# Pass 0 of a macaron block: sum over tokens on TensorE, rounding straight from PSUM, and new places for the work of all engines

## The chip, the cores and the metric

The kernel runs on one core of one Trainium2 chip. The metric is the device time of one execution in microseconds, as the median over runs. Lower is better.

## What is computed

The reference is one macaron block on x of 4 sequences with 1024 tokens and 128 features: half a feed-forward step, a mixer, and half a feed-forward step.

```python
x = x + 0.5 * ffn(layernorm(x))
x = x + attn(layernorm(x))
x = x + 0.5 * ffn(layernorm(x))
```

The feed-forward step has 8 experts of width 512. It is routed by sequence, not by token:

```python
seq_rep = hidden_states.mean(axis=1)
probs = softmax(seq_rep @ gate_w)
top_w, top_i = top_k(probs, 2)            # normalised to sum 1
hmid = gelu(hidden_states @ w1[e] + b1[e])  # for the two chosen e
out += combine[:, e] * (hmid @ w2[e] + b2[e])
```

The mixer (`attn`) is an RMS norm, a causal convolution of 4 taps, SiLU, one projection into dt, v and gate, softplus and clips of dt, a rotary turn of v, a decayed cumulative sum in chunks of 32 tokens with carries between the chunks, a mix over heads, the gate and an output projection. Everything is float32.

## The kernel before

**Passes and slots.** The two feed-forward steps of 4 sequences are 8 passes (pass q works on sequence q % 4). A pass has 8 slots: two chosen experts with four blocks of 128 hidden features each. A slot has an up product (`up`, L830: weights 128x128, z of 1024 columns) into one of two buffers `hid_ps`, a gelu on ScalarE (`gelu`, L628), and a down product into `y_ps` (`down`). The up product is made of three terms, since both factors are split into a rounded high part and the rest (`z_hi`, `z_lo`, `w1_hi`, `w1_lo`, all of the faster type float32r): 3 terms in 2 halves are 6 matmuls. The down product has three forms: by parts, with the gelu's output split too (ScalarE rounds it at L635, VectorE subtracts at L1194; 6 matmuls, L881), whole in float32 (4 matmuls, L881), and, in passes 1 to 4, with tokens as rows (L856, 16 matmuls).

**Before a pass.** VectorE takes statistics of each of the 8 tiles of 128 tokens (L1064, L1067), GpSimd adds epsilon and takes the power -0.5 (`rstd_of`, L454, L456), VectorE normalises into `f_tok` (L1079), TensorE transposes tile by tile into `aux_ps` (`turn`, L923), ScalarE copies from there to `f_tok`, whose accumulator gives the sum over tokens `zsum` (`turn_z`, L553 to L560), and rounds the copy into `z_hi` (L564); VectorE makes `z_lo` (`split_z`, L1087). VectorE widens the sum to 128 columns (`widen_sum`, L1133, L1136) so that TensorE can multiply it with the router's weights (`pre_route`, L939; L1014 in pass 0), and picks the two experts (`route`, L1143 to L1153). ScalarE, VectorE and SyncE load the two indices into registers (`value_load`); SyncE then fetches the experts' weights (`load_experts`).

In pass 0 all this stands on an idle chip. The first 256 columns of w1 of all experts are loaded ahead (`w1_all`), and ScalarE and VectorE split the first expert's from there after the register loads (`split_first`, L582, L1100); the other half comes by DMA after the index (`w1_first`, split at L598 and L1111). TensorE multiplies constants (`WARM_EARLY` = 13 products at L1009 before the first transpose, `WARM` = 5 at L1018 behind the router product), whose results nobody reads. Every float32 product with 128 weights shows as two instructions in the trace.

**The mixer** of a sequence lies between the token passes. Its names: `mixer_rms` (GpSimd's additions and the power for both norms in one operation of 16 columns, L500), `mixer_affine`, `mixer_normalise` (L1255), `mixer_residual` (eight operations on ScalarE, L673), `mixer_cos` (L1335, two halves), `mixer_decay`, `mixer_scan` and others.

**The order of work** on each engine is written out by hand or by a planner in the table `AT`: for each engine and kind of work a tick for each pass, sequence or slot. A slot has 40 ticks: `up(s)` and `gelu(s)` stand at tick 40 (s + 1), `down(s)` at 40 s + 98 or, by parts, 40 s + 132. Each engine goes through the ticks in order, and its queue is strictly in that order; the semaphores only make it wait. Before the table's first tick stand pass 0's preparation and routing. `aux_ps` is one buffer, shared by transposes, router and the mixer's products; `take_aux` makes each user wait for the last reader of the one before.

## Time and profile before

| | us |
|---|---|
| median of 3 runs | 264.93 |
| lowest and highest run | 263.94, 265.67 |
| the profiled execution, its own time | 265.42 |
| its span from the first to the last instruction | 263.6 |

Busy in the span: TensorE 96%, VectorE 84%, ScalarE 78%, GpSimd 29%. The mean granted clock of TensorE is 0.987 of full speed.

How to read it: the busy share of TensorE is that of an engine whose matmuls are pipelined, so 96% says that it seldom waited, not that it ran at its peak. The chain of waits is followed back from the last instruction to what released each step; an engine's share of it says more than its busy time. The granted clock is 1.00 at 2.4 GHz and 0.50 at 1.2 GHz. Times in the rows are counted from the start of the span.

### The profile page before, as it was taken

The numbers are of one execution on the slowest core, as the hardware profiler recorded it, in microseconds if no ns is written. First come the engines' busy times: TensorE is split into PE (matmuls) and PEld (weight loads), VectorE is DVE, ScalarE is ACT, GpSimd is POOL, SyncE is SP. The second block draws the span as 40 slices with busy tenths as digits, with TensorE's granted clock in tenths as the row PEclk, the third lists the DMA queues.
The fourth block names the chain that finished last, engine by engine and source line by source line (L and its number), as shares of the span: only waits on it lengthen the run. The fifth ranks groups of instructions, "written<-read, shape, count | busy, mean of one in ns | idle before, by whom it ended". The sixth has DMA issues, their size and how long they took to land.

```text
span 263.6 us, 4451 instructions
## 1 busy us (share of the span) xinstructions
PE 252.1 (96%) x1442; PEld 211.9 (80%) x1442; DVE 221.6 (84%) x555; ACT 204.6 (78%) x247; POOL 75.9 (29%) x84
## 2 busy tenths in 40 slices
PE   7699997999999999999999999999999999999995
PEld 6477785999979988989978999778866678887885
DVE  3668986979899998999899999899999998666632
ACT  1349899569797977877977968999989877879750
POOL 6130215550295506562015617200314004000000
PEclk9859999999999999999999999999999999999999
DMA  6589237056000061000600000600006000372022
GB/s 192 171 263 332 86 101 298 24 239 261 2 0 0 2 216 46 4 0 0 240 22 1 2 0 0 232 10 2 2 0 216 23 2 0 115 207 80 0 80 80
DMA packets 16630, 23.42 MB, mean 89 GB/s; under 512 B 1184, under 2 KB 11680, under 8 KB 16608
## 3 DMA queue, kind: packets, MB, share of 16 engines
q1 hardware_dynamic: 15296, 22.33, 25.4%
q10 hardware_dynamic: 1232, 0.55, 0.7%
q8 instruction: 11, 0.18, 0.3%
q0 software_dynamic: 80, 0.26, 0.3%
q14 instruction: 11, 0.09, 0.1%
...
## 4 chain that ended last, share of the span: by engine, by line
PE 70%; DVE 10%; issue 7%; ACT 6%; POOL 3%; DMA 1%; ACTq 1%; SPq 0%; DVEq 0%; POOLq 0%
PE hid_ps L830 27%; PE y_ps L856 18%; PE y_ps L881 12%; PE aux_ps L923 3%; PE aux_ps L970 3%; PE aux_ps L1002 2%; PE aux_ps L991 2%; POOL f_rstd L456 1%; PE aux_ps L951 1%; ACT hid L628 1%; ACT late L718 1%; DMA xt<-x_dram 1%; PE hid_ps L900 1%; DVE hid_lo L1194 1%; PE y_ps L900 1%
## 5 line engine op out<-in xcount | busy, mean ns | idle before, releaser
L830 PE MATMUL hid_ps<-z_hi,w_parts 128*128 128x512 f32 x256 | 85.4, 418 | 0.7 <-ACT w_parts L582 0.7
L628 ACT ACTIVATE hid<-hid_ps,w_sb 128x1024 f32<-128x1024 f32 x56 | 61.7, 1111 | 19.1 <-PE hid_ps L830 18.6
L856 PEld LDWEIGHTS y_ps<-w_sb,hid 128*128 128x128 f32 x512 | 61.4, 192 | 4.0 <-issue 1.2
L856 PE MATMUL y_ps<-w_sb,hid 128*128 128x128 f32 x512 | 62.6, 275 | 0.6 <-ACT hid L628 0.6
L830 PEld LDWEIGHTS hid_ps<-z_hi,w_parts 128*128 128x128 f32 x256 | 46.8, 193 | 11.6 <-issue 2.4
L830 PE MATMUL hid_ps<-z_lo,w_parts 128*128 128x512 f32 x128 | 40.9, 402 | 0.0
L1194 DVE TENSOR_TENSOR hid_lo<-hid,hid_hi 128x1024 fp32r<-128x1024 f32 x25 | 30.2, 1220 | 8.2 <-ACT hid_hi L635 8.0
L830 PEld LDWEIGHTS hid_ps<-z_lo,w_parts 128*128 128x128 f32 x128 | 24.6, 192 | 5.8
L635 ACT ACTIVATE hid_hi<-hid 128x1024 fp32r<-128x1024 f32 x25 | 26.1, 1056 | 1.5 <-PE y_ps L881 1.2
L454 POOL TENSOR_SCALAR f_ve<-f_mv 128x8 f32<-128x8 f32 (+1 forms) x9 | 4.5, 495 | 66.0 <-DVE f_mv L1067 66.0
L479 POOL TENSOR_SCALAR bias_tok<-w_sb,coef 128x128 f32<-128x128 f32 x8 | 6.2, 786 | 44.4 <-DVE coef L1163 34.1
L1079 DVE TENSOR_SCALAR f_tok<-xt,f_mv,f_rstd 128x128 f32<-128x128 f32 x64 | 17.2, 341 | 1.2 <-POOL f_rstd L456 1.2
L1064 DVE BATCH_NORM_STATS2 f_stat<-xt 128x6 f32<-128x128 f32 x64 | 13.3, 277 | 3.8 <-DMA xt<-x_dram 3.7
L1265 DVE SCALAR_TENSOR_TENSOR xc<-xs,vec_sb,xc 128x1024 f32<-128x1024 f32 x12 | 15.4, 1279 | 1.2 <-ACT xc L681 1.1
L881 PE MATMUL y_ps<-hid_hi,w_hi 128*128 128x512 f32 x50 | 16.3, 407 | 0.0
L881 PE MATMUL y_ps<-hid_lo,w_hi 128*128 128x512 f32 x50 | 15.6, 394 | 0.5 <-DVE hid_lo L1194 0.5
L881 PE MATMUL y_ps<-hid_hi,w_lo 128*128 128x512 f32 x50 | 15.6, 394 | 0.0
L456 POOL TENSOR_TENSOR f_rstd<-f_ve,neg_half 128x8 f32<-128x8 f32 (+1 forms) x9 | 14.2, 1578 | 0.8
L500 POOL TENSOR_TENSOR m_inv<-m_var,neg_half 128x16 f32<-128x16 f32 x4 | 13.8, 3446 | 0.3
L520 POOL TENSOR_SCALAR small<-mix_tmp 128x32 f32<-128x32 f32 x4 | 5.8, 1456 | 25.5 <-DVE cumd L1308 25.5
L673 ACT ACTIVATE xt<-xt,m_shift,m_gain 128x128 f32<-128x128 f32 x32 | 12.7, 482 | 0.0
L881 PEld LDWEIGHTS y_ps<-hid_lo,w_hi 128*128 128x128 f32 x50 | 9.3, 188 | 3.1 <-DVE hid_lo L1194 1.0
(143 smaller groups left out, 463.3 us busy)
## 6 DMA issues: line engine op xcount, KB each, us to landing
...
```

What stands on the lines that cost most here:

```text
L456: nc.gpsimd.tensor_tensor(f_rstd[:, tiles], f_ve[:, tiles], neg_half[:, 0, tiles], ALU.pow).then_inc(done, 1)
L500: nc.gpsimd.tensor_tensor(m_inv[:, :, :], m_var[:, :, :], neg_half[:, :, :], ALU.pow).then_inc(m_pool_step, 1)
L628: nc.scalar.activation(hid[:, slot % HBUF, :], hid_ps[:, slot % 2, :], ACT.Gelu, bias=bias).then_inc(hid_ready, 1)
L635: nc.scalar.activation(hid_hi[:, slot % 2, :], hid[:, slot % HBUF, :], ACT.Copy).then_inc(hid_hi_ready, 1)
L673: nc.scalar.activation(xt[:, b, t, :], xt[:, b, t, :], ACT.Identity, bias=m_shift[:, t:t + 1], scale=m_gain[:, t:t + 1]).then_inc(x_plus_h, 1)
L830: last = nc.tensor.matmul(hid_ps[:, slot % 2, cols], w, z[:, q % 2, cols], start=first, stop=end)
L856: last = nc.tensor.matmul(y_ps[:, cols], hid[:, slot % HBUF, cols], w_sb[:, q % 2, k, W2_AT + f * P:W2_AT + (f + 1) * P], start=t == 0 and ...
L881: last = nc.tensor.matmul(y_ps[:, cols], wt, src[:, cols], start=t == 0 and i == 0, stop=slot + 1 in (SLOTS * (q + 1), TAIL[0]) and end)
L1064: V.bn_stats(f_stat[:, t, :], xt[:, b, t, :]).then_inc(f_stats_step, 1)
L1079: V.tensor_scalar(f_tok[:, t, :], xt[:, q % B, t, :], f_mv[:, t, 0:1], f_rstd[:, t:t + 1], ALU.subtract, ALU.mult).then_inc(f_norm_done, 1)
L1194: V.tensor_tensor(hid_lo[:, slot % 2, :], hid[:, slot % HBUF, :], hid_hi[:, slot % 2, :].bitcast(F32), ALU.subtract).then_inc(hid_lo_ready, 1)
L1265: V.scalar_tensor_tensor(xc[:, :], xs[:, k:k + N], conv_w[:, k:k + 1], xc[:, :], ALU.mult, ALU.add).then_inc(conv_step, 1)
```

## The change

- **Pass 0, variance.** VectorE adds epsilon behind the statistics of each half; GpSimd only takes the two powers.
- **Pass 0, sum and transposes.** TensorE computes the sum over tokens itself: for each tile a product with the tile as weights and one column of ones, summed over the eight tiles in `y_ps`, ahead of the tile's transpose. Behind each transpose but the last stands a product of constants with 64 columns. VectorE copies the one-column sum (`keep_sum`).
- **Pass 0, z.** ScalarE rounds from PSUM into `z_hi` by halves (`turn_first`), VectorE subtracts from PSUM by halves (`split_z_first`): the first half ahead of `keep_sum`, the second behind the routing. The first up product waits for the halves one by one.
- **Register loads.** In `split_first`, ScalarE and VectorE load the second index behind the first expert's splits.
- **Passes 1 to 7.** `widen_sum` is gone: TensorE reads the sum as a broadcast. ScalarE's next turn waits for the router product instead, and VectorE's normalisation for the transposes.
- **Mixer.** GpSimd takes the power that `mixer_normalise` needs first, alone, and then the other one (5 steps in place of 4). `mixer_cos` is one operation of 1024 columns.
- **WARM** is 9 in place of 5.
- **Places.** The table `AT` is rewritten for all engines. Examples: pass 2's transposes move from 366 to 415, right behind the last down product of pass 0 (tick 412), with VectorE's normalisation from 351 to 410; the transposes of pass 0's output from 415 to 429, behind the first slot of pass 1; the splits of all experts' w1 on ScalarE from 184 and later to 290 and later; `mixer_residual` from 580, 980, 1340, 1616 to 896, 1248, 1420, 1984; `mixer_affine` of sequence 3 from 1548 to 1892; the transposes of pass 5's output from 2206 to 2326.

```diff
-        "f_norm": {1: 206, 2: 366, 3: 769, 4: 1129, 5: 1489, 6: 1860, 7: 2146},
+        "f_norm": {1: 206, 2: 415, 3: 809, 4: 1169, 5: 1469, 6: 1815, 7: 2126},
-        "y_turn_y": {0: 415, 5: 2206, 6: 2446, 7: 2600},
+        "y_turn_y": {0: 429, 5: 2326, 6: 2466, 7: 2600},
...
-        "m_residual": {0: 580, 1: 980, 2: 1340, 3: 1616},
+        "m_residual": {0: 896, 1: 1248, 2: 1420, 3: 1984},
...
-    WARM_EARLY, WARM = 13, 5
+    WARM_EARLY, WARM = 13, 9
...
-                nc.gpsimd.tensor_tensor(m_inv[:, :, :], m_var[:, :, :], neg_half[:, :, :],
+                nc.gpsimd.tensor_tensor(m_inv[:, 1, :], m_var[:, 1, :], neg_half[:, 1, :],
                                         ALU.pow).then_inc(m_pool_step, 1)
+                nc.gpsimd.tensor_scalar(m_var[:, 0, :], m_mv[:, :, 1], LN_EPS, None, ALU.add).then_inc(m_pool_step, 1)
+                pool.wait_ge(m_pool_step, POOL_STEPS * b + 3)
+                nc.gpsimd.tensor_tensor(m_inv[:, 0, :], m_var[:, 0, :], neg_half[:, 0, :],
+                                        ALU.pow).then_inc(m_pool_step, 1)
...
+            def turn_first():
+
+                act.wait_ge(f_turned_head, 1)
+                nc.scalar.activation(z_hi[:, 0, 0:HALF], aux_ps[:, 0:HALF], ACT.Copy).then_inc(zhi_head, 1)
+                act.wait_ge(f_turned, 1)
+                nc.scalar.activation(z_hi[:, 0, HALF:], aux_ps[:, HALF:], ACT.Copy).then_inc(zhi_ready, 1)
...
-                chosen.extend(act.value_load(top_i[0:1, k:k + 1], min_val=0, max_val=E - 1) for k in range(TOP))
+                chosen.append(act.value_load(top_i[0:1, 0:1], min_val=0, max_val=E - 1))
                 for f in range(HEADS):
...
+                chosen.append(act.value_load(top_i[0:1, 1:2], min_val=0, max_val=E - 1))
...
-            pre_norm(0)
+            take_aux(zlo_ready, 1, 2)
+            for t in range(NT):
+                pe.wait_ge(f_norm_done, t + 1)
+                last = nc.tensor.matmul(y_ps[:, 0:1], f_tok[:, t, :], ones[:, 0:1], start=t == 0, stop=t == NT - 1)
+                if t == NT - 1:
+                    last.then_inc(zsum_up, 1)
+                last = nc.tensor.transpose(aux_ps[:, t * P:(t + 1) * P], f_tok[:, t, :], ident[:, :])
+                if t % (NT // 2) == NT // 2 - 1:
+                    last.then_inc(f_turned_head if t < NT // 2 else f_turned, 1)
+                if t < NT - 1:
+                    nc.tensor.matmul(hid_ps[:, 0, 0:P // 2], ones[:, :], ones[:, 0:P // 2], start=True, stop=True)
             pe.wait_ge(small_in, 16)
-            pe.wait_ge(zwide_ready, 1)
-            nc.tensor.matmul(y_ps[:, HALF:HALF + E], zsum_wide[:, :], gate_sb[:, :],
+            pe.wait_ge(zsum_ready, 1)
+            nc.tensor.matmul(y_ps[:, HALF:HALF + E], zsum[:, 0:1].broadcast_to([P, P]), gate_sb[:, :],
                              start=True, stop=True).then_inc(logits_up, 1)
...
             pass_stats(0)
             pass_normalise(0)
-            widen_sum(0)
+            split_z_first(0)
+            keep_sum()
             route(0)
-            split_z(0)
+            split_z_first(1)
             split_first()
             coefficients(0)
```

## Rows read from the trace of the kernel before

**Rows 1.** The page: TensorE's granted clock in 40 equal slices, in tenths.
```profile
PEclk9859999999999999999999999999999999999999
```

**Rows 2.** Busy time by stage: stretch, length, then busy us (instructions) by engine, clock, DMA.
```profile
core 0: us, PE busy (x) PEld busy (x) DVE busy (x) ACT busy (x) POOL busy (x), PEclk, DMA share, GB/s
...
40.00:143.00 103.00, 101.24 (x672) 89.50 (x671) 93.63 (x230) 82.53 (x102) 45.05 (x44) 1.00 0.23 87
...
143.00:212.00 69.00, 66.77 (x361) 53.57 (x360) 67.02 (x149) 61.03 (x69) 17.98 (x16) 1.00 0.14 47
...
213.90:255.40 41.50, 41.46 (x199) 33.90 (x198) 27.08 (x61) 33.86 (x37) 2.80 (x2) 1.00 0.26 77
```

**Rows 3.** Chain that ended last, its start: start us, us, engine and line.
```profile
8.35 1.11 PE aux_ps L923 x4
9.49 0.70 ACT f_tok L556 x2
10.21 0.36 DVE zsum_wide L1136
10.70 0.37 PE y_ps L1014 x2
...
11.64 0.48 ACTq L579
12.40 0.28 ACTq L579
13.05 0.32 ACT w_parts L582
13.41 5.35 PE hid_ps L830 x12
...
20.48 2.75 PE hid_ps L830 x12
```

**Rows 4.** Busy time by stretch at the start, columns as in rows 2.
```profile
6.36:10.70 4.34, 2.10 (x8) 1.13 (x9) 2.58 (x9) 1.80 (x5) 1.47 (x3) 1.00 0.86 278
10.70:13.41 2.71, 2.04 (x12) 1.75 (x13) 1.61 (x5) 0.99 (x3) 0.00 (x0) 0.67 0.01 2
13.41:18.48 5.07, 5.07 (x12) 4.02 (x13) 3.96 (x26) 1.96 (x6) 1.65 (x2) 0.50 0.87 248
```

**Rows 5.** Timeline from 6 to 15 us: start us, us, engine, line, operation [idle before].
```profile
6.85 1.07 POOL L456 TENSOR_TENSOR f_rstd<-f_ve,neg_half 128x4 f32<-128x4 f32 x1
...
7.95 1.12 DVE L1079 TENSOR_SCALAR f_tok<-xt,f_mv,f_rstd 128x128 f32<-128x128 f32 x4 [0.17 <-POOL f_rstd L456]
...
11.53 1.22 DVE L1087 TENSOR_TENSOR z_lo<-f_tok,z_hi 128x1024 fp32r<-128x1024 f32 x1
...
14.70 0.42 ACT L598 ACTIVATE w_parts<-m_tok 128x256 fp32r<-128x256 f32 x1 [0.86 <-DMA m_tok<-wpack_dram]
```

**Rows 6.** Chain that ended last, near its end, where TensorE's queue is full.
```profile
222.28 0.87 PE aux_ps L923 x8
...
225.94 0.12 PE aux_ps L939 x2
```

**Rows 7.** Two lines of the kernel: duration in ns, least, median and most.
```profile
L1133 DVE TENSOR_SCALAR zsum_wide<-ones,zsum x7: 264/281/286, 28.5 to 225.0; 128x128 f32<-128x128 f32 x7
...
L1335 DVE TENSOR_TENSOR late<-aux_ps,rope_sb x8: 666/684/691, 78.5 to 193.4; 128x512 f32<-128x512 f32 x8
```

**Rows 8.** Timeline at the end of pass 0, TensorE.
```profile
44.91 1.09 PE L951 MATMUL aux_ps<-ident,yt 128*128 128x128 f32 x8 [1.36 <-ACT yt L659]
```

**Rows 9.** Around the last residual block: busy time, and ScalarE's timeline there and later.
```profile
171.00:175.00 4.00, 4.00 (x21) 2.78 (x20) 3.38 (x7) 3.89 (x11) 0.00 (x0) 1.00 0.08 30
...
171.38 3.18 ACT L673 ACTIVATE xt<-xt,m_shift,m_gain 128x128 f32<-128x128 f32 x8
...
212.79 1.21 ACT L659 ACTIVATE yt<-y_ps,bias,coef 128x1024 f32<-128x1024 f32 x1 [1.34 <-DVE bias L1206]
```

**Rows 10.** The page's groups: gelu and rounding of its output; busy us, mean ns.
```profile
L628 ACT ACTIVATE hid<-hid_ps,w_sb 128x1024 f32<-128x1024 f32 x56 | 61.7, 1111 | 19.1 <-PE hid_ps L830 18.6
...
L635 ACT ACTIVATE hid_hi<-hid 128x1024 fp32r<-128x1024 f32 x25 | 26.1, 1056 | 1.5 <-PE y_ps L881 1.2
```

250 lines of the change are left out of this document (118 added, 132 removed), and 6 rows, old and new, of the table AT.

## The prediction

> **What bounds the kernel now.** I read the page's busy shares first: TensorE is busy for nearly the whole span, and its granted clock is full except in the third and fourth of forty slices [rows 1]. Then I cut the span into stages. From 40 to 143 us TensorE works 101.2 of 103 us, from 213.9 to 255.4 us all of the time; between them, from 143 to 212 us, VectorE works 67.0 of 69 us and TensorE 66.8, so both are nearly full there, and TensorE's idle time in all three stages is only 4.0 us [rows 2]. What happens in those stages is therefore mostly a queue that is worked off: a matmul that starts earlier at the front lets the end come earlier by the same amount, unless VectorE or ScalarE stops it on the way.
>
> The front is different. In the chain of waits the first expert matmul starts at 13.41 us, behind a serial relay: transpose, ScalarE's copy with its sum, VectorE's widening, the router product, the index, two register loads, ScalarE's rounding of the first weights [rows 3]. And the clock is at its lower level, 1.2 GHz, for all of the first twelve expert matmuls: 0.67 on average from 10.70 to 13.41 us, 0.50 until 18.48 us, and 1.00 before and after [rows 4]. These twelve take 5.35 us; twelve of the same kind take 2.75 us from 20.48 us on, at 2.4 GHz [rows 3]. Before the fall TensorE had been busy 2.10 of 4.34 us, with eight transposes and nothing else [rows 4]. So the start holds two things that a change could win: the relay, and 2.6 us of low clock. The low digits of the clock stand in the trace of this one execution; in others the fall may stand elsewhere.
>
> **The change, part by part.**
>
> *Variance plus epsilon on VectorE in pass 0.* GpSimd's own addition and its two hand-overs go; its two powers then stand nearly back to back. The second power starts at 6.85 us today [rows 5] and ends 1.07 us later; the first ends about 6.55 us. With one more small operation on VectorE ahead of each power I expect the last normalised tile 0.2 us earlier, at 8.85 us in place of 9.07 us (7.95 + 1.12) [rows 5]. The bounds are 0 and 0.3 us.
>
> *The sum over tokens on TensorE, products as fill.* Each of eight tiles now costs TensorE a one-column product with the tile as weights (two instructions, as every f32 product here), the transpose, and a 64-column product (two instructions). Eight transposes take 0.87 us in a full queue, so 0.11 us each; a two-instruction product of 8 columns adds 0.12 us [rows 6]. A product with 1 column I take at 0.12 us, one of 64 columns at 0.12 us as well (bounds 0.12 and 0.22 us, from the 8-column row and from two instructions of 128 columns at the transposes' pitch). That makes 0.35 us a tile, where VectorE delivers one each 0.28 us (1.12 / 4) [rows 5]. TensorE becomes the slower of the two: from about 6.95 us, 8 x 0.35 - 0.12 = 2.7 us later, the last tile's sum and transpose have been issued (9.65 us), and they are out at about 9.8 to 9.9 us. Today the last transpose is out at 9.46 us (8.35 + 1.11) [rows 3]. So this part by itself makes the transposes 0.4 us later (0 to 1.0 us later with the bounds), and pays it back in the relay: ScalarE's 0.70 us and the 128-wide widening of 0.36 us [rows 3] leave the path, and a copy of one column (about 0.2 us with its hand-over, as the small chain steps) takes their place. The router product then starts at 9.8 + 0.2 + 0.14 = 10.1 us in place of 10.70 us. VectorE's first half of the low part, about 0.68 us like the other 128x512 reads of PSUM [rows 7], stands ahead of that copy in its queue; it needs ScalarE's rounding of the first half, and ends at about 9.8 us, just as the sum does. That is the closest race of this step: if it is late, the router is late by as much. The second half, after the routing operations, ends by about 11.7 us, before the matmuls want it.
>
> *Rounding straight from PSUM.* ScalarE no longer copies z and then rounds it, and no longer reads an accumulator. This is hidden: two activations of 512 columns, about 0.60 us each without the accumulator's read, end at about 10.5 us, and the matmuls start later than that.
>
> *The second register load moved behind the first weights.* From 11.64 us to 12.40 us ScalarE's queue has one register load, from 12.40 us to 13.05 us the other, and then the rounding starts [rows 3]. The later one leaves the path: 0.65 us. From the router product on, the relay is 0.94 us to the load (11.64 - 10.70), 0.76 us for it, 0.36 us to the matmul (13.41 - 13.05), so the first expert matmul starts at 10.1 + 0.94 + 0.76 + 0.36 = 12.2 us: 1.2 us earlier. The load itself then stands before the first bias copies, which only the first gelu needs.
>
> *Four more constant products behind the router.* Eighteen instructions at 0.11 us are 2.0 us, so from 10.3 to 12.3 us at full clock: they just fill the gap and may cost 0.1 us. At half clock they would take twice that (see the rivals).
>
> *The clock.* After the change TensorE has a gap of about 0.6 us around 6.4 to 7.0 us, another short one at 9.9 us, and work at all other times from 1.7 us on. Today its longest thin stretch is the one before the fall: 2.10 of 4.34 us from 6.36 us, then nothing of length until 10.9 us [rows 4]. I take it that the clock now stays at 2.4 GHz. Then the twelve matmuls run from 12.2 to 14.95 us. What is late next is ScalarE: it waits for the rest of the first expert's weights until 14.70 us today [rows 5], and that transfer follows the index, so 14.1 us; 0.42 us for the rounding [rows 5] and 1.11 us for the first gelu [rows 10] make 15.65 us; the first down product takes 1.72 us (20.48 - 18.76, where 18.76 is the end of the twelve) and ends at 17.4 us. Today it ends at 20.48 us [rows 3]. **Gain at the start: 3.0 us**; without the clock 1.2 us. The later weights, which VectorE waited for today ahead of its other splits, are waited for after them in the new order, so I see no stall of the size of the gain behind this.
>
> The Trainium skill ("TensorE: Matmul & The Clock Gate", Part 4: PE-mode transpose) says that a transpose doesn't count as busy for the clock. The trace agrees as far as it goes: the fall came after a stretch that held transposes only. By that rule the sum would get less help from the new mix, where transposes are a third of the time; that is the second case below.
>
> *The end of pass 0.* TensorE idles 1.36 us for the scaled output, which ScalarE makes in 1.21 us [rows 8, 9]. The transposes of pass 2 (0.87 us) now stand right there, and those of the output go behind the first token slot. The transposes are gated by VectorE's normalisation, which is placed there too (twice 1.12 us for eight tiles [rows 5]), so they will not fit wholly into the hole: 0.4 us, bounds 0 and 0.87 us.
>
> *Widening gone in passes 1 to 7, cosine in one piece.* Seven operations of 281 ns are 2.0 us of VectorE, and per batch two of 684 ns become one of about 1.22 us, 0.15 us less [rows 5, 7]. The broadcast read of the sum costs TensorE nothing new. Only where VectorE is full does this count: two widenings and one or two cosines lie between 143 and 212 us. 0.6 us, bounds 0 and 1.2 us.
>
> *The mixer's power in two.* VectorE's normalisation then waits for a power of 8 columns in place of one of 16, and two steps sooner. In the two stages where the mixer runs VectorE idles 11.4 us in all [rows 2], and the waits list none of it for this power, so by itself it gives nothing (lower bound); GpSimd, busy 29% of the span, hides what it costs. Its worth is the freer placement.
>
> *The rewritten places.* Nearly every tick moves. Most move by a slot or less, with their consumers. Of size: the residual blocks, eight operations, 3.18 us of ScalarE in one piece [rows 9], go later by 316, 268, 80 and 368 ticks (a slot has 40). I count the rest at nothing, between 1.5 us better and 1.5 us worse.
>
> The sum: 3.0 + 0.4 + 0.6 = 4.0 us. The profiled execution took 265.42 us, so 261.4 us. It lies 0.5 us above the median of the runs (264.93 us), whose own start I can't see; I predict **261.2 us**. About 1%, or 2.65 us, is what a measurement of this kernel can tell from no change.
>
> **The rivals.**
>
> *A. The forecast*, 261.2 us, 50%, with 259.3 to 262.8 us around it from the bounds of the terms.
>
> *B. The clock falls anyway near the first expert matmuls.* Only the 1.2 us of the relay remain: 264.9 - 1.2 - 1.0 = 262.7 us. For it: the one-column products and the short fill stream few columns, and the mean of 0.67 puts today's fall near 11.6 us, while the five products ran [rows 4]. Against it: TensorE has hardly a gap left. 20%.
>
> *C. The clock falls before the nine products.* Then the fill itself is in the way: 18 x 0.21 = 3.8 us from 10.3 to 14.1 us, the twelve end at 14.1 + 5.35 = 19.45 us, 0.7 us later than the 18.76 us of today. With the 1.0 us from elsewhere: 264.6 us. The full clock in the thin stretch of today's run speaks against it. 10%.
>
> *D. The gain is swallowed between 143 and 212 us.* VectorE idles 2.0 us in 69 there [rows 2]; if its order, not TensorE's, sets the path, only what VectorE itself starts earlier is kept. Against it: it idles 9.4 us in the 103 us before, so it can come forward with TensorE. Half of the start lost: 262.8 us. 12%.
>
> *E. Slower: the residual blocks stall TensorE.* ScalarE needs 1.1 us for the gelu and 1.1 us for the split [rows 10] against TensorE's 2.8 us a slot (twice the 1.37 us of six matmuls), so a block of 3.18 us in one slot can leave TensorE waiting up to 3.18 - 0.6 = 2.6 us, and there are four. It decides from 1.0 us each on (that eats the 4.0 us). Full price 264.9 - 4.0 + 4 x 1.8 = 268.1 us, with 1.8 us for a slot whose gelu is a little ahead. Against it: around today's last block TensorE is busy 4.00 of 4.00 us [rows 9], and the last one now goes near 212 us, where ScalarE idles 1.34 us by itself [rows 9]; it also leaves ScalarE's full stretch. 8%.
>
> **How the numbers follow.** A has 50%, B 20%, D 12%, C 10%, E 8%. The range 259.2 to 265.2 us holds A, B, D, C, without E and the tails. Faster by over 1% means below 262.3 us: most of A and a third of B and D, 0.6. Within 1%: 0.32. Slower by over 1% (267.6 us): 0.08.
>
> **What the profile would show.** Right: first expert matmul at 12.2 us; granted clock 1.00 from 5 to 20 us and the first twelve in 2.8 us; first down product finished near 17.4 us; TensorE idle less than 1.0 us around the end of pass 0; the end of the matmuls of pass 7 some 4 us earlier. Wrong: clock below 1.00 between 9 and 18 us (B, C); TensorE idle over 6 us from 40 to 255 us (D, E); ScalarE as the releaser of long waits beside the residual blocks (E); the router product later than 10.4 us, if the PSUM halves or the one-column products cost more than taken.

## The result and the profile after

| | us |
|---|---|
| before, median of 10 runs beside the change | 264.68 |
| after, median of 10 runs | 267.39 |
| after, lowest and highest run | 264.88, 268.00 |
| after, the profiled execution, its own time | 265.35 |
| its span | 263.6 |

The ratio of after to before is 1.0091, with a 95% interval from 1.0062 to 1.0120. The change makes the kernel slower by 0.9%, where 1.4% faster was forecast.

One property of the runs is needed for every number below. Executions of one kernel differ in their mean granted clock: 1.000, 0.993 or 0.987 of full speed, because a fall of the clock happens in some executions and not in others. I call them "at full clock", "at 0.993" and "at 0.987". Medians of all executions, us (number of executions):

| | full clock | 0.993 | 0.987 |
|---|---|---|---|
| before (118 executions, run beside the experiments) | 263.43 (15) | 264.38 (39) | 265.12 (64) |
| after | 265.12 (2) | 266.49 (3) | 267.80 (5) |

So the change loses 1.7 us at equal full clock (by only two executions of after), and 2.7 us where both have the lowest mean. The profiled execution of after is one of the two at full clock, and the profiled one of before has 0.987. Two traces with nearly the same own time (265.35 and 265.42 us) therefore hide a difference of 1.7 us.

The page of after: span, busy time by engine, and the clock in 40 slices.

```profile
span 263.6 us, 4512 instructions
...
PE 254.0 (96%) x1480; PEld 214.1 (81%) x1480; DVE 221.3 (84%) x547; ACT 203.6 (77%) x244; POOL 78.9 (30%) x86
...
PEclk9999999999999999999999999999999999999999
```

The clock stays full at the start, where it fell before [rows 1]. The front in stretches: busy us (instructions) by engine, then the granted clock.

```profile
core 0: us, PE busy (x) PEld busy (x) DVE busy (x) ACT busy (x) POOL busy (x), PEclk, DMA share, GB/s
6.36:10.70 4.34, 4.04 (x41) 3.88 (x40) 3.04 (x10) 0.60 (x1) 1.19 (x2) 1.00 0.92 300
10.70:13.51 2.81, 2.63 (x25) 2.47 (x24) 1.24 (x6) 1.03 (x3) 0.00 (x0) 1.00 0.04 13
13.51:18.20 4.69, 4.39 (x19) 2.84 (x18) 3.55 (x24) 3.39 (x9) 0.88 (x2) 1.00 0.74 195
```

Against [rows 4] the clock is 1.00 in all three. The first twelve expert matmuls run from 13.51 to 16.52 us, so 3.0 us in place of 5.35 us [rows 3]. The first down product has its last matmul out at 18.78 us in place of 20.48 us:

```profile
15.91 0.61 PE L831 MATMUL hid_ps<-z_hi,w_parts 128*128 128x512 f32 x2
16.82 1.96 PE L882 MATMUL y_ps<-hid,w_sb 128*128 128x512 f32 x4 [0.30 <-ACT hid L625]
```

But the first of them starts at 13.51 us, not 1.2 us earlier than the 13.41 us of before. The relay up to it, from the timeline (start us, us, engine, line, operation, and in brackets the idle time before and its releaser):

```profile
10.98 0.16 DVE L1154 COPY zsum<-y_ps 128x1 f32<-128x1 f32 x1 [0.55 <-PE y_ps L1012]
...
11.28 0.36 PE L1022 MATMUL y_ps<-gate_sb,zsum 128*128 128x8 f32 x2 [0.18 <-DVE zsum L1154]
...
11.96 0.17 DVE L1167 FIND_INDEX8 top_i<-top_v,y_ps 128x8 uint32<-128x8 f32 x1
...
13.08 0.51 ACT L578 ACTIVATE w_parts<-late 128x128 fp32r x2 [1.34 <-DVE top_i L1167]
...
13.51 0.71 PE L831 MATMUL hid_ps<-z_hi,w_parts 128*128 128x512 f32 x2
```

The router product starts at 11.28 us; before it started at 10.70 us [rows 3], and 10.1 us was forecast. The second register load is gone from the way as expected: from the index (12.13 us) to the rounding are 0.95 us. From the router product to the first expert matmul it is 2.23 us; before it was 2.71 us (10.70 to 13.41), and 2.06 us was forecast. What ate the gain lies ahead of the router: the eight tiles. TensorE's groups there, one row for each line of code (busy us, mean ns of one, idle before):

```profile
L1012 PE MATMUL y_ps<-ones,f_tok 128*128 128x1 f32 x16 | 2.7, 238 | 0.3 <-DVE f_tok L1093 0.3
L1015 PE MATMUL aux_ps<-ident,f_tok 128*128 128x128 f32 x8 | 2.5, 306 | 0.0
L1019 PE MATMUL hid_ps<-ones 128*128 128x64 f32 x14 | 2.3, 248 | 0.0
```

These are 2.7 + 2.5 + 2.3 = 7.5 us of overlapping busy time in 4.1 us. The timeline shows the pitch: the transposes start at 7.24, 7.75, 8.25, 8.76 us and so on, 0.51 us apart, where I had 0.35 us. Within a tile the one-column product takes 0.20 us of it (7.55 to 7.75), the transpose 0.14 us (to 7.89) and the 64-column product 0.17 us (to 8.06).

Then the middle. The longest single piece of TensorE's idle time and what leads to it:

```profile
82.49 4.34 POOL L519 TENSOR_SCALAR small<-mix_tmp 128x32 f32<-128x32 f32 x1 [2.73 <-DVE cumd L1325]
...
86.93 0.41 POOL L520 TENSOR_SCALAR ncd<-cumd 128x32 f32<-128x32 f32 x1
...
87.42 2.04 POOL L523 TENSOR_TENSOR small<-ncd 128x31 f32<-128x31 f32 x1
...
89.55 0.26 ACT L728 ACTIVATE small_e<-small 128x64 f32<-128x64 f32 x1 [2.93 <-POOL small L523]
...
91.12 1.11 ACT L625 ACTIVATE hid<-hid_ps,w_sb 128x1024 f32<-128x1024 f32 x1
...
92.38 2.02 PE L857 MATMUL y_ps<-w_sb,hid 128*128 128x128 f32 x16 [2.98 <-ACT hid L625]
```

TensorE waits 2.98 us for a gelu. The gelu waits in ScalarE's queue behind a small operation of the mixer's decay (L728), which waits 2.93 us for GpSimd, whose first operation here took 4.34 us.

### The profile page after: what moved, and what is told of

It is laid out like the page before. It is cut to its first block, busy times and chain, and to the rows that moved or that the text cites. A ratio compares the mean times of both kernels' runs of the same rounds, so it can differ in the third digit from the quotient of the medians.

```text
span 263.6 us, 4512 instructions
## 1 busy us (share of the span) xinstructions
PE 254.0 (96%) x1480; PEld 214.1 (81%) x1480; DVE 221.3 (84%) x547; ACT 203.6 (77%) x244; POOL 78.9 (30%) x86
## 4 chain that ended last, share of the span: by engine, by line
PE 43%; DVE 8%; issue 3%; DVEq 0%
PE hid_ps L831 16%; PE y_ps L882 12%; PE y_ps L857 6%; PE aux_ps L968 3%; PE aux_ps L924 2%; PE aux_ps L989 1%; PE hid_ps L901 1%; PE y_ps L901 1%; PE aux_ps L949 1%; DVE xc L1282 1%; DVE late L1383 1%; DVE m_tok L1272 1%; PE aux_ps L1000 1%; DVE xt L1400 1%; DVE f_stat L1072 1%
## 5 line engine op out<-in xcount | busy, mean ns | idle before, releaser
L831 PE MATMUL hid_ps<-z_hi,w_parts 128*128 128x512 f32 x256 | 83.8, 411 | 0.0
L831 PEld LDWEIGHTS hid_ps<-z_hi,w_parts 128*128 128x128 f32 x256 | 46.1, 189 | 11.0 <-issue 2.4
L831 PE MATMUL hid_ps<-z_lo,w_parts 128*128 128x512 f32 x128 | 40.0, 394 | 0.0
L1211 DVE TENSOR_TENSOR hid_lo<-hid,hid_hi 128x1024 fp32r<-128x1024 f32 x25 | 30.3, 1220 | 10.2 <-ACT hid_hi L632 10.1
L831 PEld LDWEIGHTS hid_ps<-z_lo,w_parts 128*128 128x128 f32 x128 | 24.0, 188 | 5.6
L463 POOL TENSOR_SCALAR f_ve<-f_mv 128x8 f32<-128x8 f32 x7 | 1.7, 249 | 64.8 <-DVE f_mv L1075 64.6
L453 POOL TENSOR_TENSOR f_rstd<-f_ve,neg_half 128x8 f32<-128x8 f32 (+1 forms) x9 | 15.0, 1663 | 2.6 <-DVE f_ve L1079 1.9
L519 POOL TENSOR_SCALAR small<-mix_tmp 128x32 f32<-128x32 f32 x4 | 7.7, 1920 | 26.2 <-DVE cumd L1325 26.2
L475 POOL TENSOR_SCALAR bias_tok<-w_sb,coef 128x128 f32<-128x128 f32 x8 | 7.6, 958 | 17.7 <-DVE coef L1180 17.5
L882 PEld LDWEIGHTS y_ps<-hid_hi,w_lo 128*128 128x128 f32 x50 | 9.4, 188 | 2.3
```

The costliest lines, as they stand in the source:

```text
L453: nc.gpsimd.tensor_tensor(f_rstd[:, tiles], f_ve[:, tiles], neg_half[:, 0, tiles], ALU.pow).then_inc(done, 1)
L831: last = nc.tensor.matmul(hid_ps[:, slot % 2, cols], w, z[:, q % 2, cols], start=first, stop=end)
L882: last = nc.tensor.matmul(y_ps[:, cols], wt, src[:, cols], start=t == 0 and i == 0, stop=slot + 1 in (SLOTS * (q + 1), TAIL[0]) and end)
L1211: V.tensor_tensor(hid_lo[:, slot % 2, :], hid[:, slot % HBUF, :], hid_hi[:, slot % 2, :].bitcast(F32), ALU.subtract).then_inc(hid_lo_ready, 1)
```

## Experiments

The runs ask four things: what the clock at the start is worth, what the new relay costs and gives, which of the new places lose the rest, and how. "New table" is the `AT` of after, "old table" that of before. For every kernel I give the ratio to before with its interval, and medians at equal clock where that decides.

**1. The table against the code.** `old_table` is the changed code with the old table. `new_table` is the code of before with the new table (and the widening placed just ahead of each routing).

```diff
-AT = {...of after...}
+AT = {...of before...}        # old_table
```


> All code of the changed kernel, but the table of places is that of the kernel before. Theory P (the places lose it: ScalarE's decay step of sequence 0, placed ahead of a gelu, waits 2.9 us for GpSimd, and TensorE then idles 3.0 us at 89 us, in every execution): the stall is gone; TensorE idles under 1 us from 80 to 100 us, and the kernel is 2 to 3 us faster than the changed one, ratio to before 0.995 to 1.000. Theory F (the front loses it: five weight loads a tile, and a low clock after it): nothing of the 2.7 us against before comes back; ratio to before 1.005 to 1.015, as with the new places.

> All code of the kernel before, but the table of places is the changed one (the widening, which that table lacks, is placed a few ticks ahead of each router product). Theory P: slower than before by about the stall less the 0.9 us that the end of pass 0 gives, ratio 1.005 to 1.012, and TensorE idles 2.5 to 3.5 us near 90 us. Theory F: within 0.3% of before.

`old_table`: 264.79 us (264.03 to 265.54, 12 runs), ratio 1.0009 [0.9984, 1.0034], 11 of 12 at full clock. `new_table`: 267.78 us (266.29 to 268.76, 6 runs), ratio 1.0121 [1.0080, 1.0162]. In the medians the new places alone, on unchanged code, make the whole loss. The changed code with old places loses nothing and wins nothing, although its clock is held, which alone is worth more than a microsecond (experiment 4). At equal clock it has a loss of its own: 264.76 us at full clock against 263.43 us of before, and after is only 0.4 us above that. So at full clock the new places cost the changed code little on balance (experiment 6 shows good and bad blocks in them); what they add is mostly that 8 of 10 executions fall below full clock, against 1 of 12 with the old places. On the code of before the new places cost more: 266.73 us (two executions) against 264.38 us at 0.993.

The stall of 2.98 us isn't needed for this loss. In `new_table` the same decay operation stands ahead of the same gelu, but GpSimd's first operation takes 2.40 us and TensorE waits 0.34 us for the gelu; that expectation failed. Its longest waits behind the first expert matmuls are for the widened sum (waits of TensorE, us in total, times, longest):

```profile
PE aux_ps L939 <- DVE zsum_wide L1133: 1.2, 2, 0.8
PE y_ps L856 <- ACT hid L628: 0.3, 1, 0.3
```

In the trace of `old_table` TensorE waits in pass 0 for a split on VectorE that in the old table stands behind the bias of the down product (tick 107 ahead of 112). The bias reads the down product's weights, which are fetched at that time; the row of the bias itself names no releaser, so that it waits for this transfer is argued, not shown:

```profile
19.28 0.21 DVE L1222 TENSOR_SCALAR bias2a<-w_sb,coef 128x1 f32<-128x1 f32 x1 [1.79 <-issue]
...
20.14 1.20 PE L832 MATMUL hid_ps<-z_hi,w_parts 128*128 128x512 f32 x4 [0.38 <-DVE w_parts L1134]
```

**2. The decay of sequence 0 behind the gelu.** One number: ScalarE's decay from tick 830 to 860, with gelu(20) at 840.

```diff
-        "m_decay": {0: 830, 1: 1100, 2: 1533, 3: 1906},
+        "m_decay": {0: 860, 1: 1100, 2: 1533, 3: 1906},
```


> The changed kernel with one number changed: ScalarE's decay step of sequence 0 at tick 860 in place of 830, so behind the next slot's gelu. Theory P: the wait for GpSimd remains, but no gelu stands behind it; TensorE idles under 1 us near 90 us; 2 to 3 us faster than the changed kernel, ratio to before 0.997 to 1.002. Rival R (the path then runs on through the same late decay step to the scans, and VectorE, not TensorE, sets the end): less than 1 us comes back. Theory F: nothing comes back.

265.52 us (264.69 to 266.24, 12 runs), ratio 1.0038 [1.0014, 1.0061]. The wait of 2.98 us is gone. The clock is full in 9 of 12 executions (2 of 10 in after) and never at 0.987. But at full clock the median is 265.43 us, not below after's 265.12 us. The gelu no longer waits; instead the mixer's own scan is late and TensorE waits for that (waits of TensorE, us in total, times, longest):

```profile
PE aux_ps L1000 <- DVE late L1391: 1.2, 1, 1.2
PE aux_ps L989 <- DVE late L1383: 0.8, 1, 0.8
```

So the stall costs nothing that its cure gives back at equal clock: the two traces end the last matmul at the same 260.71 us. Its price is the clock: after with the stall falls to 0.993 or 0.987 in 8 of 10 executions, without it 3 of 12 fall, to 0.993.

**3. Without the seven products behind the tiles** (`no_fill`), to test the 0.51 us a tile and the clock.

```diff
-                if t < NT - 1:
-                    nc.tensor.matmul(hid_ps[:, 0, 0:P // 2], ones[:, :], ones[:, 0:P // 2], start=True, stop=True)
```


> The changed kernel without the seven constant products between the transposes. Theory F1 (weight loads set the pitch: 0.51 us a tile for five): 0.34 us a tile for three, so the last sum is ready 1.1 us earlier and the first expert matmul starts at 12.4 us in place of 13.5 us; 1 us faster at the same clock. Theory F2 (the fill holds the clock up): the clock falls in all executions, for longer than now, mean granted clock 0.986 or less, and the median is not better than that of the changed kernel.

265.58 us (265.12 to 267.01, 12 runs), ratio 1.0053 [1.0027, 1.0080]. A tile now takes 0.29 us, which is VectorE's pace (0.28 us), and the first expert matmul starts at 12.28 us, 1.23 us earlier than in after: two weight loads less for each of seven tiles. At a mean of 0.993 it is 1.2 us faster than after (265.30 against 266.49 us). But no execution has a full mean. In the profiled one the clock holds at the start and falls right behind the stall:

```profile
86.00:91.13 5.13, 2.14 (x10) 1.50 (x9) 4.54 (x5) 3.01 (x4) 1.99 (x1) 0.99 0.63 195
91.13:94.54 3.41, 3.41 (x17) 3.41 (x17) 2.90 (x3) 3.41 (x6) 0.00 (x0) 0.52 0.53 212
94.54:98.00 3.46, 3.46 (x25) 2.97 (x23) 1.28 (x1) 3.46 (x10) 0.65 (x3) 1.00 0.00 0
```

TensorE was busy 2.14 of 5.13 us, then ran 3.41 us at about the lower level while it was full of work, and rose again. Each such fall costs about 1.4 us here (after: 265.12, 266.49 and 267.80 us for none, one and two steps of mean clock). Where the eight lower executions of after fall isn't shown, since its profiled one has the full clock. And the start isn't safe without the seven products: in the profiled executions of `early` and `mixed_no_fill` (experiments 5 and 6), which leave them out too, the granted clock is 0.50 from 10.8 to 14.2 us.

**4. Only constant products added to before** (`before_filled`): seven of 64 columns between pass 0's transposes, three of 128 columns behind them, nine behind the router in place of five.

```diff
+                    if head_done is not None and t < NT - 1:
+                        nc.tensor.matmul(hid_ps[:, 0, 0:P // 2], ones[:, :], ones[:, 0:P // 2], start=True, stop=True)
...
+            for _ in range(3):
+                nc.tensor.matmul(hid_ps[:, 0, 0:P], ones[:, :], ones[:, :], start=True, stop=True)
             pe.wait_ge(small_in, 16)
             pe.wait_ge(zwide_ready, 1)
```


> The kernel before, all places and the relay as they were, with constant products alone added: seven of 64 columns between pass 0's transposes, three of 128 behind them, and nine in place of five behind the router product. Theory C (the clock is worth what the executions of before say: 263.5 us at a mean clock of 0.999 or 1.000, 265.2 us at 0.987): the clock is full in most executions and the median is 263.4 to 264.0 us, ratio to before 0.995 to 0.998, better than all the changed code with the old table. Theory N (the full clock is worth no more than the 0.6 us seen with the changed code): 264.5 to 265 us.

263.70 us (263.34 to 264.03, 10 runs), ratio 0.9957 [0.9936, 0.9977], all ten at full clock. This is the cleanest price of the clock at the start. Before's own executions at full clock and at 0.987 differ by 265.12 - 263.43 = 1.7 us; `before_filled` is 1.4 us under before at 0.987. The twelve matmuls are stretched by more, 2.3 us (5.35 less 3.0). Both traces start the first expert matmul at 13.41 us, and from slot 4 on `before_filled` stands 1.8 to 1.9 us ahead of before's trace, to the end. I use it as the reference at full clock from here on.

**5. New places in front, old ones behind.** `mixed` takes a place from the new table only where both tables have it at tick 600 or earlier; `mixed_no_fill` leaves out the seven products too, and `old_no_fill` is the old table without them.

> The changed kernel, with its new places only where the old and the new tick are both at or below 600 (pass 0 and 1), and the old places behind. Theory S (the new places of pass 0 win, the ones behind put VectorE's scan of sequence 0 ahead of the convolution of sequence 1 and lose it again): the first 20 slots are 2 to 2.5 us earlier than before, as in the changed kernel, and at least 1 us of it is kept to the end; ratio to before 0.990 to 0.997. Theory M (the mixer's chain sets the end in any order, and the front can't move it): no more than 0.3 us at slot 24 and at the end; ratio 0.998 to 1.003.

> As before this, and without the seven constant products between the transposes. Both theories: the first expert matmul 1.1 us earlier. Theory S: 0.5 to 1.1 us faster than with them, ratio to before 0.986 to 0.994. Theory M: the same end as with them.

> The changed code with the old table of places and without the seven products between the transposes. Theory G (weight loads on TensorE's path are what the front paid): 1.0 us earlier from slot 0 on, the clock still at its full level in most executions since the stall at 89 us isn't there, and 0.5 to 1.0 us faster than with the products; ratio to before 0.996 to 0.999. Theory K (without the products the clock falls at the start in most executions, as before the change): mean clock 0.987 to 0.993 in most, no faster than before.

| | median, us (range, runs) | ratio to before | at full clock |
|---|---|---|---|
| `mixed` | 265.95 (265.19 to 266.49, 12) | 1.0052 [1.0030, 1.0074] | 265.81 |
| `mixed_no_fill` | 264.17 (263.81 to 265.59, 12) | 0.9978 [0.9958, 0.9998] | 263.99 |
| `old_no_fill` | 263.71 (263.25 to 264.27, 11) | 0.9963 [0.9943, 0.9983] | 263.61 |

The seven products cost 1.2 us with the old table (264.76 less 263.61) and 1.8 us with the mixed one: what they delay at the start stays to the end. `mixed` was a miss: I expected it to keep the start's gain, and it waits for VectorE in the slots 16 to 19, where new and old places meet. A table of places can't be halved at a tick without new waits at the seam; `mixed` measures its seam too.

**6. One block of places at a time.** All without the seven products. `order_back`: the new table with the old order of sequence 0's scan and sequence 1's convolution. `early`: the old table, with new places only up to tick 250. `early_end`: `early` and in addition the new places at the end of pass 0. `early_two`: `early` with products behind tiles 4 and 6, 14 in place of 13 products ahead of the tiles and 7 in place of 9 behind the router. `new_behind`: `early` in front, old places up to 600, new places behind. `output_first`: the new table, but pass 0's output transposes ahead of the first slot of pass 1 as before.

```diff
# early_end against early
-        "f_norm": {1: 206, 2: 366, ...
+        "f_norm": {1: 206, 2: 415, ...
-        "y_turn_y": {0: 415, ...
+        "y_turn_y": {0: 429, ...
...
# output_first against no_fill
-        "y_turn_y": {0: 429, ...
+        "y_turn_y": {0: 415, ...
```


> The changed kernel without the seven products between the transposes and with all its new places, but for sequence 0's decay exponential, scans, gate, heads, output and sequence 1's clip, first tap and convolution, which have the old ticks: so the convolution of sequence 1 stands ahead of the scan of sequence 0 again, and the decay step behind the gelu. Theory O (that order lost the 3 us between slots 20 and 24): no stall of 3 us, and slot 24 starts at least 2 us earlier than in the same kernel with the new order at its full clock; 1.0 to 2.5 us faster than it (265.3 us at 0.993, 266.9 us at 0.987), ratio to before 0.990 to 0.998. Theory M (the mixer's chain as a whole): slot 24 within 0.5 us of where it is now; then only the lower clock behind the stall comes back, 264.0 to 264.5 us.

> The changed code without the seven products, the old places, but the new ones where both ticks are at or below 250: VectorE's bias of pass 0, which waits for the second half of the weights, stands behind the splits that the next up products need. Theory W (in the old table that wait ate the 1.0 us that the shorter relay gave: slot 0 was 1.06 us earlier than with the relay of before, slot 4 0.03 us): slot 4 is 0.8 to 1.0 us earlier than in before_filled, and it lasts: 262.7 to 263.1 us at full clock. Theory L (something behind it, as the low parts or the loads, holds slot 4): as old_no_fill, 263.6 us.

> As early, and with the new places at the end of pass 0: pass 2's transposes in TensorE's wait for the scaled output, the output's transposes behind the first slot of pass 1. Theory P2 (time that TensorE wins is kept): slot 10 is 0.8 us earlier than in early, and so is the end. Theory M (the first update of x is 1 us later by it, and the mixer's chain hangs on that): slot 10 earlier, but slot 24 no earlier than in early, or up to 1 us later.

> As early, with two of the seven products back (behind the fourth and the sixth tile), 14 in place of 13 products ahead and 7 in place of 9 behind. Theory H (a product costs two weight loads of about 0.085 us, and a few of them hold the clock): 0.34 us later than early at the full clock, but at the full clock in nearly all executions, so that the two medians are within 0.3 us. Rival: the clock falls as often as without them, and it is slower by 0.3 us.

> The changed code without the seven products; old places where both ticks are at or below 600 (but the early ones of the kernel called early), new places behind. Theory B (the places behind tick 600 lose it): slot 24 at +1.5 to +2.5 us against before_filled at the full clock, 265 us or more. Theory A (the places of the end of pass 0 lose it, since the update of x is late): the stall apart, slot 24 at +0.5 us or less at the full clock, 262.7 to 263.7 us.

> The changed kernel without the seven products, with three ticks changed: the output's transposes ahead of pass 2's and of the first slot of pass 1, as in the old table, and VectorE's update and statistics right behind. Theory A: statistics of the mixer 1.5 to 3 us earlier (45 us in place of 46.65 us), TensorE 0.5 to 1.5 us later at slot 10, and slot 24 earlier than in the same kernel without this, by 1 us or more. Theory B: slot 24 as now or later.

| | median, us (range, runs) | ratio to before | full clock | 0.993 |
|---|---|---|---|---|
| `order_back` | 265.57 (264.10 to 267.38, 12) | 1.0021 [0.9994, 1.0047] | 264.15 | 265.75 |
| `early` | 262.93 (262.39 to 264.19, 7) | 0.9924 [0.9897, 0.9952] | 262.68 | 264.09 |
| `early_end` | 267.39 (265.88 to 268.81, 6) | 1.0097 [1.0058, 1.0135] | 265.88 (one) | 267.28 |
| `early_two` | 263.39 (262.93 to 263.52, 8) | 0.9940 [0.9916, 0.9964] | 263.39 | |
| `new_behind` | 265.70 (264.28 to 267.25, 12) | 1.0041 [1.0015, 1.0067] | 264.38 (two) | 265.70 |
| `output_first` | 267.51 (266.19 to 268.54, 6) | 1.0099 [1.0064, 1.0135] | 266.19 (one) | 267.51 |

What follows:

- The new places up to tick 250 are good: they undo the wait of `old_table` (splits ahead of the bias), 263.61 to 262.68 us at full clock.
- The new places behind tick 600 cost 1.7 us at full clock (262.68 to 264.38) and bring the stall of 2.5 to 3.0 us back, and the clock's falls with it: 2 of 12 executions at full clock, against 5 of 7 in `early`.
- `early_two` holds the clock in 8 of 8 executions, as expected, but costs 0.7 us at full clock (262.68 to 263.39), where 0.34 us was expected for its four weight loads. The rest isn't explained.
- The order of scan and convolution is not it: `order_back` at 0.993 has 265.75 us and `no_fill` 265.30 us.
- The late output transposes of pass 0 are not it either: moving them back costs `no_fill` 2.2 us more at 0.993. That expectation failed.
- The end of pass 0 can't be moved alone. In `early_end` TensorE waits for the normalisation in the middle of its transposes, 2.09 us, the clock falls behind it in the profiled execution, and at equal mean clock the kernel is 3.2 us slower than `early` (265.88 against 262.68 us, 267.28 against 264.09 us). In after the same places stand among neighbours that were moved with them and save 0.8 us of idle time (below).

```profile
43.48 0.99 PE L920 MATMUL aux_ps<-ident,f_tok 128*128 128x128 f32 x3 [2.09 <-DVE f_tok L1087]
```

**7. What the relay is worth.** `early_gap` is `early` with two constant products between the last transpose and the router product. `relay_early` is `before_filled` (old relay, VectorE widens the sum) with the table of `early`.

```diff
# early_gap
+            for _ in range(2):
+                nc.tensor.matmul(hid_ps[:, 0, 0:P], ones[:, :], ones[:, :], start=True, stop=True)
             pe.wait_ge(small_in, 16)
             pe.wait_ge(zsum_ready, 1)
```


> As early, with two constant products between the last transpose and the router product, where TensorE waits 0.4 us for the copy of the sum. If the clock falls for want of work there: the full clock in nearly all executions at no cost of path, 262.6 to 262.9 us. If not: clock as in early (two of seven below full), and up to 0.1 us later.

> The kernel called before_filled (sum by ScalarE and VectorE, clock held by products) with the early places of the kernel called early. If the sum on TensorE and the rest of the short relay are worth the 1.1 to 1.2 us that slot 0 shows: about 263.6 us, 0.8 us slower than early_gap at the full clock. If the loads of weights set the first slots: within 0.2 us of early_gap.

`early_gap`: 262.51 us (262.48 to 264.01, 8 runs, all at full clock), ratio 0.9925 [0.9899, 0.9950]. `relay_early`: 263.32 us (263.19 to 264.39, 11 runs, all at full clock), ratio 0.9940 [0.9921, 0.9960]. With the same places and the same clock, the changed code as a whole is worth 0.8 us in the medians. That isn't the relay alone: `relay_early` also lacks the saved operations of VectorE and the cosine in one piece. The first expert matmul starts at 12.36 us, 1.05 us earlier than in `before_filled`. `early_gap` is the fastest kernel of all, 0.75% under before and 1.8% under after.

The traces show a loss inside it. From slot 4 to slot 18 `early_gap` is 1.2 us ahead of `relay_early`, from slot 19 on only 0.85 us. Between them stand the transposes before pass 3, which need `aux_ps` and wait for the cosine that reads it. `early_gap` (cosine in one operation) and then `relay_early` (in two halves):

```profile
77.55 1.09 PE L920 MATMUL aux_ps<-ident,f_tok 128*128 128x128 f32 x8 [0.94 <-DVE late L1346]
...
78.24 1.25 PE L919 MATMUL aux_ps<-ident,f_tok 128*128 128x128 f32 x8 [0.41 <-DVE late L1335]
```

The second half of the cosine no longer hides behind the first transposes. `old_table` has the wait of 0.9 us too, before and `before_filled` have 0.4 us.

**8. Transposes beside their normalisation.** At full clock, what remained open was 1.8 us. I cut the traces of after and `before_filled` into the same stretches; only TensorE's column is used (us, busy us). After:

```profile
13.50:46.00 32.50, 31.97 (x151) 24.42 (x150) 27.40 (x99) 27.66 (x40) 7.14 (x8) 1.00 0.61 195
46.00:80.00 34.00, 34.00 (x231) 30.81 (x231) 29.78 (x83) 23.92 (x26) 17.58 (x18) 1.00 0.35 125
80.00:102.00 22.00, 19.02 (x126) 16.22 (x125) 19.51 (x31) 18.16 (x25) 7.44 (x6) 1.00 0.25 80
...
140.00:175.00 35.00, 34.62 (x221) 29.62 (x219) 34.58 (x87) 30.00 (x36) 19.37 (x15) 1.00 0.13 46
175.00:212.00 37.00, 36.46 (x173) 28.41 (x174) 36.13 (x69) 35.04 (x43) 6.18 (x8) 1.00 0.13 44
```

`before_filled`:

```profile
13.50:46.00 32.50, 31.14 (x147) 23.66 (x147) 28.39 (x94) 28.69 (x43) 9.05 (x8) 1.00 0.67 224
46.00:80.00 34.00, 33.59 (x228) 29.97 (x228) 29.81 (x91) 25.26 (x33) 17.46 (x16) 1.00 0.26 98
80.00:102.00 22.00, 22.00 (x150) 19.44 (x149) 20.81 (x37) 19.20 (x25) 7.46 (x10) 1.00 0.25 80
...
140.00:175.00 35.00, 34.19 (x222) 29.65 (x221) 33.81 (x83) 29.50 (x38) 12.11 (x12) 1.00 0.13 46
175.00:212.00 37.00, 35.61 (x164) 26.82 (x163) 36.20 (x71) 33.14 (x36) 6.06 (x5) 1.00 0.12 44
```

Idle time of TensorE goes down at the end of pass 0 (1.36 to 0.53 us), down behind it (0.41 to 0), up at the stall (0 to 2.98 us), down where VectorE is full (0.81 to 0.38 and 1.39 to 0.54 us). Together, with the stretches left out here, it is 4.5 us against 4.0 us: only 0.5 us more. Yet from the first expert matmul to the end of the last matmul after takes 247.20 us and `before_filled` 245.41 us. The rest is busy time of a kind: transposes that follow a normalisation tile by tile. After, ahead of pass 7:

```profile
219.08 2.15 DVE L1093 TENSOR_SCALAR f_tok<-xt,f_mv,f_rstd 128x128 f32<-128x128 f32 x8 [1.56 <-POOL f_rstd L453]
...
219.57 2.04 PE L924 MATMUL aux_ps<-ident,f_tok 128*128 128x128 f32 x8
```

and `before_filled`:

```profile
218.58 2.15 DVE L1083 TENSOR_SCALAR f_tok<-xt,f_mv,f_rstd 128x128 f32<-128x128 f32 x8 [0.36 <-POOL f_rstd L456]
...
220.20 1.03 PE L923 MATMUL aux_ps<-ident,f_tok 128*128 128x128 f32 x8
```

Eight transposes take 2.04 us beside the normalisation and 1.03 us behind it, and no row counts the difference as idle. From the first weight load to the start of the last transpose the blocks before the passes 2, 5 and 7 take 1.38, 1.30 and 1.88 us in after, and 1.02, 1.02 and 1.03 us in `before_filled`: 1.5 us more. With the 0.5 us of idle time that is 2.0 us, against 1.79 us measured.

Where the time goes by place shows in the starts of the slots (the first matmul of the up product), taken where all tables have the same work behind them: us later than in `before_filled`, each from its one trace. `new_table` alone has a fall of the clock in it, at the start.

| | slot 8 | slot 18 | slot 24 | slot 52 | slot 54 | last matmul |
|---|---|---|---|---|---|---|
| `before_filled`, us | 35.14 | 75.34 | 102.03 | 217.42 | 223.99 | 258.83 |
| after | 0.6 | -0.5 | 2.0 | 0.7 | 2.0 | 1.9 |
| `decay_later` | 0.7 | -0.4 | 1.6 | 0.7 | 1.9 | 1.9 |
| `new_table` | 1.2 | 0.9 | 1.9 | 2.5 | 3.8 | 3.7 |
| `old_table` | 1.1 | 1.1 | 1.5 | 1.3 | 1.3 | 1.3 |
| `early_gap` | -0.4 | -0.4 | 0.0 | -0.2 | -0.2 | -0.2 |

After wins 1.1 us at the end of pass 0, loses 2.5 us between the slots 18 and 24, wins 1.3 us back by slot 52 and loses 1.2 us at the transposes before pass 7.

Two runs test the largest one. `turn_ahead` is `early_gap` with the transposes before pass 7 ahead of a down product; `turn7_later` is `decay_later` with them behind it.

```diff
-        "f_norm": {..., 6: 1860, 7: 2146},
+        "f_norm": {..., 6: 1860, 7: 2126},     # turn_ahead
...
-        "f_norm": {..., 6: 1815, 7: 2126},
+        "f_norm": {..., 6: 1815, 7: 2146},     # turn7_later
```


> Taken from the version that is so far the fastest (the short relay, two constant products behind the last transpose, new places only up to tick 250), with one number changed: TensorE's transposes before pass 7 stand at tick 2126 in place of 2146, so ahead of a down product and not behind it. In the trace of the kernel after, these eight transposes took 1.88 us from first weight load to last matmul, because VectorE normalises the eight tiles in 2.15 us at the same time and TensorE follows tile by tile; with the old place they took 1.03 us. Theory: such stretched transposes are lost time of TensorE that no row shows as idle, so this kernel is 0.6 to 0.9 us slower than 262.5 us: 263.1 to 263.4 us. Rival: TensorE only runs ahead of its queue there and the time comes back at the next wait for ScalarE or VectorE: 262.5 us, unchanged within 0.2 us.

> The changed kernel with the decay of sequence 0 behind the gelu (tick 860), and in addition with the transposes before pass 7 back behind the down product (TensorE 2126 to 2146, ScalarE's turn 2140 to 2144). With the decay moved alone it took 265.4 us at full clock. Theory: the transposes then take 1.0 us in place of 1.88 us and the whole is 0.6 to 0.9 us faster: 264.5 to 264.8 us at full clock. Rival: the wait goes to ScalarE's turn, the routing and pass 7's first slot, which now start later by as much: 265.4 us, unchanged within 0.2 us.

`turn_ahead`: 264.31 us (263.75 to 264.95, 10 runs, all at full clock), ratio 0.9991 [0.9969, 1.0013]. The one number costs 1.8 us against `early_gap` in the medians. In the traces 1.3 us arise between slots 52 and 54; another 0.4 us are there already at the first expert matmul, which the edit doesn't touch. The executions agree: the fastest five of `turn_ahead` take 263.75 to 263.99 us, six of the eight of `early_gap` 262.48 to 262.52 us, 1.3 us apart. That is more than the 0.85 us of the stretch, because the stretch leaves out the time before the first weight load. Counted from start to start, six matmuls and the eight transposes take 3.45 us in `turn_ahead` (217.62 to 221.07) and 2.19 us in `early_gap` (218.60 to 220.79):

```profile
219.28 2.03 PE L920 MATMUL aux_ps<-ident,f_tok 128*128 128x128 f32 x8
221.07 0.71 PE L878 MATMUL y_ps<-hid_hi,w_hi 128*128 128x512 f32 x2
```

`turn7_later` was a miss in the other direction: 266.85 us (266.38 to 267.70, 4 runs, all at full clock), ratio 1.0106 [1.0060, 1.0153], 1.4 us slower than `decay_later`. Its transposes take 1.0 us, but TensorE now waits at the down product ahead of them:

```profile
218.72 2.15 DVE L1093 TENSOR_SCALAR f_tok<-xt,f_mv,f_rstd 128x128 f32<-128x128 f32 x8 [1.56 <-POOL f_rstd L453]
...
222.05 0.73 PE L882 MATMUL y_ps<-hid_lo,w_hi 128*128 128x512 f32 x2 [1.78 <-DVE hid_lo L1211]
```

In the new table VectorE's normalisation (tick 2111) stands ahead of the low part of the gelu (2139) that this product reads; in the old one (2128) it stands behind it (2114). The stretched transposes are real lost time, but their cause is VectorE's place as much as TensorE's, and only the pair can be moved.

## Why the prediction was wrong, step by step

**The sum.** Forecast 4.0 us gained; measured 2.7 us lost in the medians. Against the 264.9 us it started from, the terms came out like this:

| term | forecast | shown |
|---|---|---|
| relay up to the first expert matmul | 1.2 | -0.1 |
| low clock of the first twelve matmuls | 1.8 | 1.7 |
| end of pass 0 | 0.4 | 0.8 of idle time |
| VectorE between 140 and 212 us | 0.6 | 1.3 of idle time |
| the rewritten places | 0 (1.5 either way) | -3.0 idle, -1.5 stretched |
| falls of the clock (taken as none) | none | up to -2.7, in 8 of 10 executions |

The column of what was shown isn't a sum: idle time at one place isn't lost time at the end (`decay_later`).

**The tiles of pass 0: the term was mis-sized.** I took a tile at 0.35 us, from transposes at 0.11 us and a small product at 0.12 us. It is 0.51 us, the five weight loads of a tile at about 0.1 us each: both the one-column product and the 64-column product load 128x128 weights twice, and the number of columns hardly matters. My upper bound, "0 to 1.0 us later with the bounds", didn't reach the 1.6 us by which the last transpose came later (11.1 us in place of 9.46 us). The three parts were taken at 0.12, 0.11 and 0.12 us (one-column product, transpose, 64-column product) and are 0.20, 0.14 and 0.17 us: I had priced the two products by a single 8-column product behind eight transposes [rows 6], not by a queue in which each of them follows another kind of work. The mechanism was right: without the seven products the same relay starts the expert matmuls 0.9 to 1.1 us earlier than before (`old_no_fill` 12.48, `early_gap` 12.36, `no_fill` 12.28 us), which is close to the forecast 1.2 us, and at equal places and clock the changed code is worth 0.8 us at the end. The second register load left the path, but from the router product on 0.48 us were saved, where 0.65 us was forecast.

**The low clock: right in kind and nearly in size.** The clock held at 1.00 and the first twelve took 3.0 us. Rivals B and C fall for the profiled execution. I had read 2.75 us for twelve such matmuls at full clock from a chain [rows 3], so the stretch was 2.3 us and not 2.6 us. I kept 1.8 us of it behind ScalarE's weights and gelu; before's own executions show 1.7 us, and `before_filled` 1.4 us. What the page of before couldn't show is that 0.987 is only the commonest of three cases, so that a change that holds the clock is compared with a mixture. The Trainium skill ("TensorE: Matmul & The Clock Gate", Part 4: PE-mode transpose) says that transposes don't count as busy for the clock. The runs agree as far as they go: constant products between and behind the same transposes kept the clock in ten of ten executions, where before lost it in 103 of 118. They can't tell this from the mere amount of work, since the products also filled the idle time.

**The end of pass 0: right in sign, and for a reason that I didn't give.** The idle time from 13.5 to 46 us fell by 0.8 us, within the bounds 0 and 0.87 us, and by the slots 1.1 us were won. But as a single move it costs 3.2 us (`early_end`). I had named the gate (VectorE's normalisation is placed there too) and then priced it as a hole partly filled. The same gate appears before pass 5 and pass 7 as stretched transposes, which I didn't look for.

**VectorE's saved operations:** idle time of TensorE between 140 and 212 us fell by 1.3 us, above the 0.6 us and slightly above its bound of 1.2 us. The gain hangs on the places: from slot 24 to slot 52 after wins 1.3 us on `before_filled`, `old_table` with the same code 0.2 us, and `new_table` with the same places loses 0.7 us. The cosine in one piece wasn't only a gain: with the old places it costs 0.5 us of waiting for `aux_ps` before pass 3 (experiment 7). The sum had priced VectorE's side of it and not who waits for the buffer.

**The mixer's power in two** gave nothing that a run shows, as forecast. It wasn't tried alone.

**The rewritten places: the step that failed.** I wrote "I count the rest at nothing, between 1.5 us better and 1.5 us worse". `new_table` shows that these places alone cause a loss as large as the whole. I had picked the residual blocks by size (3.18 us of ScalarE) for rival E. They stall nothing: between 13 and 262 us after's trace has one wait of TensorE above 0.5 us, the one for the gelu behind the decay. The mechanism of rival E was right, an operation of the mixer ahead of a gelu in ScalarE's strict queue, but its carrier was an operation of 0.26 us that waits for another engine. Size was the wrong thing to look for; the question was what the moved operation waits for. Its gelu stands 10 ticks behind it. GpSimd's first operation of the decay took 1.2 to 1.8 us before and 4.34 us here. But this stall is the visible part of the loss and not the whole mechanism: `new_table` loses 3 us without it.

**Rival D** (the gain is swallowed between 143 and 212 us) is refuted: after stands at slots 10 to 18 0.5 us ahead of `before_filled`, the loss comes in slots 19 to 24 and before pass 7, and between them it wins. Its price was also added up wrongly: half of the start's 3.0 us lost and 1.0 us kept from elsewhere make 262.4 us, not 262.8 us.

**What I took for nothing: the clock in mid-kernel.** A new stall was priced by its length. At full clock, its cure gives back nothing (`decay_later`, 265.4 us), so the mixer's chain sets the same end without the stall. But the clock falls, in `no_fill` and `output_first` right behind the stall with a full queue waiting, and one or two steps of mean clock cost after 1.4 to 2.7 us. This is why the median of after is 2.3 us above its own best case.

**Still open.** How much of the loss between slots 19 and 24 belongs to which of the moved mixer operations is not settled: `decay_later` and `order_back` each exclude one candidate, and no run isolates the rest. `new_table` loses only 1.0 us there, but 0.7 us more up to slot 52, where after wins; why the new places cost the code of before most, no run shows.
